# Attend in two halves, with the fourth projection between them, in a pipelined transformer kernel

## What is computed

```python
q, k, v = split(x @ Wqkv)              # 16 heads of 64
q, k = rotary(l2norm(q)), rotary(l2norm(k))
sim  = q @ k.T * 8                     # blocks of 32 tokens, each sees itself and the block before
attn = softmax(where(mask, -max, sim))
x = x + (attn @ v) @ Wo
a, g = split(layernorm(x) @ W1 + b1)
x = x + (a * gelu(g)) @ W2 + b2
```

## Time and profile before

| | us |
|---|---|
| median of 3 runs (4521.66 to 4527.89) | 4525.05 |
| the profiled execution's own time | 4522.37 |
| its span, first to last instruction | 4520.3 |
| PE busy / DVE busy / POOL busy / ACT busy | 3896.4 / 3136.0 / 2356.6 / 2228.0 |

### The profile page before, as it was taken

One profiled execution on the slowest core, in us unless ns is written; L12 is line 12 of the kernel. 1 busy time (PEld: TensorE's weight loads), 2 busy tenths in 40 slices (PEclk: granted clock), 3 DMA queues, 4 the chain that ended last, 5 costly groups with the idle time before them and its releaser, 6 DMA issues.

```text
span 4520.3 us, 149223 instructions
## 1 busy us (share of the span) xinstructions
PE 3896.4 (86%) x67429; PEld 2666.5 (59%) x67429; DVE 3136.0 (69%) x5129; ACT 2228.0 (49%) x3263; POOL 2356.6 (52%) x1644
## 2 busy tenths in 40 slices
PE   6999999768888888888888888888888888888886
PEld 4776777635555555555555555555555555555555
DVE  4445444557777777777777777777777777788884
ACT  3111111435555556665556665555556565555553
POOL 2101010156656666666666666666666666666662
PEclk8999999989999999999999999999999999999997
DMA  3101010000000000000000000000000000000000
GB/s 146 57 38 57 38 57 38 1 6 8 9 10 11 23 21 10 9 10 23 22 9 9 10 23 20 10 9 9 22 23 10 10 10 19 19 16 13 13 12 13
DMA packets 50654, 98.35 MB, mean 22 GB/s; under 512 B 11611, under 2 KB 40678, under 8 KB 45542
## 3 DMA queue, kind: packets, MB, share of 16 engines
q1 hardware_dynamic: 49286, 88.42, 6.2%
q10 hardware_dynamic: 736, 0.40, 0.0%
HBM read 61.25 MB, written 2.36 MB: 14 GB/s over the span
## 4 chain that ended last, share of the span: by engine, by line
PE 40%; DVE 16%; issue 10%; ACT 7%; POOL 5%; DMA 1%; SPq 0%; DVEq 0%; POOLq 0%; ACTq 0%
PE pQ L1723 11%; PE pW L1745 7%; PE pC L1820 6%; ACT sq L1584 4%; PE pW L1706 4%; DVE n L1451 4%; PE pC L1830 3%; PE pM L1785 3%; DVE m L1439 3%; DVE rot L1429 3%; POOL rot L1308 3%; DVE PT L1419 2%; PE pW L1785 2%; PE pW L1771 2%; DVE hh L1484 2%
## 5 line engine op out<-in xcount | busy, mean ns | idle before, releaser
L1316 POOL TENSOR_TENSOR rot<-rot,m 128x1024 f32<-128x1024 f32 x384 | 907.1, 2362 | 598.7 <-DVE m L1439 598.2
L1584 ACT ACTIVATE sq<-pQ 128x1024 f32<-128x1024 f32 x380 | 389.4, 1025 | 847.6 <-PE pQ L1723 814.1
L1308 POOL TENSOR_TENSOR rot<-rot,rn 128x1024 f32<-128x1024 f32 x384 | 729.0, 1910 | 7.5
L1451 DVE TENSOR_REDUCE n<-sq 128x16 f32<-128x1024 f32 x380 | 461.5, 1214 | 373.4 <-ACT sq L1584 373.4
L1745 PE MATMUL pW<-PT,V 32*64 32x64 f32 x24576 | 322.8, 235 | 213.9 <-issue 213.9
L1429 DVE TENSOR_TENSOR rot<-pQ,tabl 128x1024 f32<-128x1024 f32 x380 | 459.6, 1209 | 57.0 <-ACT sq L1584 55.9
L1439 DVE TENSOR_TENSOR m<-pQ,tabl 128x1024 f32<-128x1024 f32 x380 | 461.6, 1215 | 5.3 <-POOL rot L1316 5.2
L1745 PEld LDWEIGHTS pW<-PT,V 32*64 32x64 f32 x24576 | 294.1, 135 | 262.9 <-issue 262.9
L1723 PE MATMUL pQ<-wk,xs 128*128 128x512 f32 x760 | 422.1, 684 | 5.8 <-DVE m L1439 4.8
L597 POOL TENSOR_TENSOR b_xcT<-b_cB,b_xT 128x2048 f32<-128x2048 f32 x16 | 72.2, 4515 | 604.3 <-DMA b_cB<-b_crow 604.3
L1723 PE MATMUL pQ<-wq,xs 128*128 128x512 f32 x760 | 377.7, 620 | 6.2 <-DMA xs<-XT 3.3
(11 more groups left out here) (238 smaller groups left out, 7038.1 us busy)
## 6 DMA issues: line engine op xcount, KB each, us to landing
b_cB<-b_crow SPq DMA_DIRECT2D x32, 1024.0 KB, 5.9
xs<-XT SPq DMA_DIRECT2D x192, 64.0 KB, 2.4
ys<-XT SPq DMA_DIRECT2D x192, 64.0 KB
wq<-in_wqkv SPq DMA_DIRECT2D x6, 512.0 KB, 3.6
wk<-in_wqkv SPq DMA_DIRECT2D x6, 512.0 KB, 4.9
wv<-in_wqkv SPq DMA_DIRECT2D x6, 512.0 KB, 4.8
wo<-in_wo SPq DMA_DIRECT2D x6, 512.0 KB, 5.4
w<-in_w SPq DMA_DIRECT2D x6, 384.0 KB, 3.8
```

Of the source, the lines that this page charges most:

```text
L1308: e.tensor_tensor(r, r, rn[b % 2][:, c:c + HEADS].unsqueeze(2).to_broadcast([P, HEADS, HD]), ALU.mult)\
L1316: e.tensor_tensor(rot[j % RING][:, :], rot[j % RING][:, :], m2[:, :, :].rearrange("p h d -> p (h d)"), ALU.add)\
L1451: e.tensor_reduce(n2[:, c:c + HEADS], heads(squared(j)), AX.X, ALU.add).then_inc(v_red.sem, 1)
L1584: e.activation(squared(j), projected(j), ACT.Square).then_inc(a_sq.sem, 1)
```

## The change

`attend` gets a part number, and its 8 blocks of tokens are written as four parts of two. Parts 0 and 1 stand where attend stood; then come `hidden(C, 2)` and `project(A, 3)` as before; parts 2 and 3 follow, ahead of `turn(R, "2b")`. All of attend's waits stay with part 0, its signal `p_pv` goes with part 3. The instruction of `at_rest` goes away. `scores` gets parts too, but its two parts follow each other, so that nothing moves there.

```diff
-            def attend(n):
+            def attend(n, part):
                 if n is None:
                     return
-                if n:
-                    e.wait_ge(v_wo.sem, v_wo.at("xa", n - 1))
...
-                free(1)
-                at_rest(e)
-                for v in range(NW):
+                if part == 0:
+                    if n:
+                        e.wait_ge(v_wo.sem, v_wo.at("xa", n - 1))
+                    e.wait_ge(a_v.sem, a_v.passed(n + 1))
+                    e.wait_ge(v_tt.sem, v_tt.at("tt", 2 * n + 1))
+                    if n + 1 < NP:
+                        e.wait_ge(v_s.sem, v_s.at("su", 2 * n + 3))
+                    free(1)
+                    bank[1] = (a_ov, "1", n)
+                for v in range(2 * part, 2 * part + 2):
...
-                x.then_inc(p_pv.sem, 1)
-                bank[1] = (a_ov, "1", n)
+                if part == 3:
+                    x.then_inc(p_pv.sem, 1)
...
                 hidden(C, 1)
-                attend(Dn)
+                attend(Dn, 0)
+                attend(Dn, 1)
                 hidden(C, 2)
                 project(A, 3)
+                attend(Dn, 2)
+                attend(Dn, 3)
                 turn(R, "2b")
                 combine(Dn)
```

More of the change, by code:

```diff
@@ L1694, in _, with scores @@
             e.wait_ge(g_set, GSET)
-            def scores(n, g):
+            def scores(n, g, part):
                 if n is None:
@@ L1699, in scores @@
                 q, k = qT[n % 2], kT[n % 2]
[L1700 to L1703, removed]
+                if part == 0:
+                    if g == 0:
+                        e.wait_ge(a_tr.sem, a_tr.passed(n + 1))
+                    e.wait_ge(a_mask.sem, a_mask.at("mk", 2 * n + g))
+                for w in range(4 * part, 4 * part + 4):
                     for j in range(4):
@@ L1709, in scores @@
                                          skip_group_check=True, tile_position=(HD * s, 32 * j))
-                x.then_inc(p_s.sem, 1)
+                if part:
+                    x.then_inc(p_s.sem, 1)
             def project(n, u):
@@ L1843, in _ @@
             for A, R, B, Dn, C, F in passes():
-                scores(B, 0)
+                scores(B, 0, 0)
+                scores(B, 0, 1)
                 project(A, 0)
@@ L1854, in _ @@
                 normed(C)
-                scores(B, 1)
+                scores(B, 1, 0)
+                scores(B, 1, 1)
                 values(R, 3)
```

## The result

The changed kernel takes 4378.44 us, the median of 3 runs (4377.0 to 4382.97), against 4525.05 before: a ratio of 0.968, 95% interval 0.9661 to 0.9699.

The account below looks back on a forecast made before the run. PE was taken to be bound by code waits in attend, heading the chain to `contract`. Terms -79, -44, +13 and +13 give -97 us: 4522.4 becomes 4425, or 4428 for the median; range 4385 to 4495.

Parts of the forecast that it names:

- What bounds the end of a pass: Attend, fourth projection, `square(A, 3)`, DVE's work and `contract` form a chain; `contract` idles 1.77 us for DVE.
- The gaps are waits for code, and the second goes: Attend's 213.9 us of gaps await 256-instruction blocks needing about 3.5 us; boundaries 4.4 us apart remove the second half's.
- The first gap stays: The gap in attend's first half remains, since nothing moves ahead of it: some 35 passes, 1.24 us each.
- The price of the bare `heads_out`: At attend's end, `project` no longer covers `heads_out`; the square follows 2.02 us after attend's last result.
- Pass by pass: Attend's start to `contract`: 14.48 us without a first gap, 15.84 and 15.59 in the two worked passes with one.
- Scores are the same. What is left is where half of attend stands.: Splitting `scores` into parts moves nothing, so only the place of attend's second half was priced.
- cost nothing by themselves: PE's new waits for `heads_out`, at the transposes and `combine`, add no time; PE is done at 6.6, `contract` comes at 8.52.
- `at_rest` costs nothing that shows.: Removing this instruction at attend's start gains nothing, since attend starts with no idle time before it.
- Together: Sum over all passes, all of it from attend's start to `contract`: -97 us, with no change from `contract` on.
- The clock rival: Idling 1.9 us ahead of `contract` halves the clock there in four passes of ten: 65 us back, 4493; chance 0.18.
- Attend's own gaps: Something in attend, not code, stops it, so the second gap stays: +80 us, 4605; chance 0.09.
- Nothing comes of it: Another engine sets the next pass's start, and a shorter tail becomes a longer wait there: 4525; chance 0.07.

Follow-up runs that it names:

- e4: The changed kernel with `square(A, 3)` ahead of `heads_out` on ACT; 4264.26 us, ratio 0.9426 to the kernel before.
- e3: The changed kernel with only `hidden(C, 2)` between the halves of attend, the fourth `project` again behind the second half; 4334.83 us, ratio 0.9586.
- e6: The changed kernel with the whole of attend behind `hidden(C, 2)` and `project(A, 3)`, so early project without the split; 4687.97 us, ratio 1.0392.
- f1: The changed kernel measured again, unedited, on another chip beside three further runs; 4386.54 us, ratio 0.9704.
- f2: The changed kernel with `at_rest` put back in its old place behind attend's waits; 4400.38 us, ratio 0.9733.
- e2: The kernel before without `at_rest`, nothing else changed; 4512.08 us, ratio 0.9977.
- f4: The kernel before without `at_rest`, measured a second time on another chip; 4503.68 us, ratio 0.997.
- e7: The changed kernel with `square(A, 3)` ahead of `heads_out` on ACT, and DVE's `squares(A, 3)` and `hidden(C, 2)` ahead of `probs(B, 0)`; 4232.6 us, ratio 0.9385.
- e5: The kernel before, attend whole, with `square(A, 3)` ahead of `heads_out` on ACT, so `combine` waits for `heads_out`; 4705.76 us, ratio 1.0432.

## Why the prediction was right in its way and short in its size

- **What bounds the end of a pass.** Right: the chain of attend, squares, DVE and `contract`. e4 shows it by cutting the chain.
- **The gaps are waits for code, and the second goes.** Right: 95 gaps in the second half became 4, e3's shrink to what was left over, e6's are back, and before's end 1.18 to 1.59 us behind a packet of code. The Trainium skill, "Runtime: NRT & Kernel Launch", section "Instruction fetch mechanics", calls a crossing mostly hidden; the changed kernel's second half agrees with that, where 4.4 us of work lie between boundaries, and before, e3 and e6 do not.
- **The first gap stays.** Right in number: 34 of them after, 35 before.
- **The price of the bare `heads_out`.** This is a term of the sum that was mis-sized: 2.02 forecast, 1.86 measured in nearly all passes, 0.16 x 95 = 15 us more gain. I had let the squares begin 0.04 behind the copies' end; they begin 0.12 before it (3755.99 against 3754.17 + 1.94).
- **Pass by pass.** 14.31 median without a first gap (14.48 forecast), 15.44 with one (15.6 to 15.8 forecast), 15.59 in the last layer's (15.77): each off by about the same 0.16.
- **"Scores are the same. What is left is where half of attend stands."** This step failed. The scores were not moved, but the gaps in the first of them changed, 32.9 to 12.0 us: 21 us, the largest part of what is missing. PE's new waits were said to "cost nothing by themselves"; that they could bring something was not thought of, because only what is queued behind a wait was followed, and not the code that is fetched around it.
- **"`at_rest` costs nothing that shows."** This failed too: about 14 us by f1 and f2, 12 to 15 by e2 and f4. That attend starts with no idle time before it was not enough to price it at nothing.
- **Together.** In the traces the tail lost 1.31 us a pass, 124 us in all, and the rest 0.22, 21 us. Forecast were 97 and 0. Of the 27 more in the tail 15 are `heads_out`. The other 12 are about `at_rest`'s 14 in size, but that they are the same is not shown: f1, the same kernel once more, has a tail of 14.91 in place of 14.80, some 10 us in all, and first gaps of 43.3 us in place of 38.8 (forecast 35 x 1.24 = 43). On f1's chip the gain is 4518.96 - 4386.54 = 132 us, about what the forecast, `heads_out` and the scores add up to (97 + 15 + 21 = 133). Where `at_rest`'s 14 stand in that sum stays open.
- **The clock rival.** The clock did fall ahead of `contract`: in 19 of 94 passes `combine` took over 3.9 us. There it was covered, as the prediction had it for that place; behind `contract`, where the rival had put it, it was at full for 3.5 us in all 94. PE's timeline of the changed kernel at such a place, and below it a stretch within this `combine`, with its granted clock of 0.50 (1.2 GHz):

```profile
2307.22 5.41 PE L1763 MATMUL pW<-oT,wo 128*128 128x256 f32 x16 [0.20 <-ACT oT L1604]
...
2313.56 1.56 PE L1833 MATMUL pC<-hh,w 128*128 128x256 f32 x6
```

```profile
2308.40:2310.00 1.60, 1.60 (x5) 1.23 (x5) 1.60 (x3) 1.60 (x3) 0.00 (x0) 0.50 0.00 0
```

`combine` takes 5.41 in place of 3.72, and `contract` starts 6.34 after `combine`'s start, as in the pass shown above (3762.50 - 3756.16). The idle 1.75 ahead of `contract` has swallowed it.
- **The other two rivals.** Attend's own gaps fell with the changed kernel itself, where 4 of 95 were left in the second half, and with e3. "Nothing comes of it" fell with the rest of a pass, which did not grow (19.88 against 20.11).

## What to carry to other kernels

Where many small matmuls follow each other, look for waits with no releaser at a fixed distance in instructions: large matmuls put between two such places shorten or remove them, and how much is needed can be read from the gap itself (here about 3.5 us to a block: with 2.5 us, 1.0 was left, with 4.4 hardly any). When work is moved to make room, follow what it had been covering: the fourth `project` hid `heads_out`, and taking the squares off that bare piece, with DVE's order to match (e7), brought the ratio from 0.968 to 0.9385, about as much again as the split. And when a change adds or removes a wait or an empty instruction, don't price it by the idle time in front of it alone.

## What the runs showed that was not expected

- With a new wait, later code arrived in time: with PE waiting for `heads_out` at `combine`, the first scores' gaps went from 32.9 us to 12.0, and in e5 to 1.9. Ahead of the gaps that stayed, the packet of code came 1.0 to 1.8 us after the release of the wait at `contract`.
- An instruction that does nothing cost about 14 us in 96 passes in one place, and nothing that shows in another.
- The clock fell to half in `combine` (5.41 us) with no idle time longer than 1.21 us on PE just ahead of it, whereas the pass shown with 1.75 us idle ahead of `contract` ran `contract` at its usual 1.56.
